# Diagonal masks of the transposed causal scores: from VectorE to TensorE in every third head group

## What is computed

```python
xn1 = layernorm(x, g1, be1)
q, k, v = heads(xn1 @ Wq + bq), heads(xn1 @ Wk + bk), heads(xn1 @ Wv + bv)   # 16 heads of 32
scores = einsum('bhtd,bhsd->bhts', q, k) / DH ** -0.5
scores = where(tril(ones(1024, 1024)), scores, -inf)      # causal
sa = einsum('bhts,bhsd->bhtd', softmax(scores), v)
x = x + (sa @ W1 + b1)
x = x + cross_attention(layernorm(x), ctx) @ W2 + b2       # 64 context rows, no mask
x = x + relu(layernorm(x) @ Wf1 + bf1) @ Wf2 + bf2
out = layernorm(x + gate(x) * routed_vision(x))            # fusion stage
```

## Time and profile before

| | us |
|---|---|
| runs | 2347.75, 2347.81, 2345.16; median 2347.75 |
| profiled execution: span, first to last instruction | 2338.9 |
| median less span | 8.85 |
| TensorE busy | 2198.0 (94%) |
| VectorE busy | 1410.1 (60%) |
| POOL busy | 933.6 (40%) |
| ScalarE busy | 868.2 (37%) |
| mask additions on VectorE (L1011), 512 | 138.3 |

### The profile page before, as it was taken

The page is one execution under the profiler, slowest core; times in us unless marked ns, Lnnn a source line. Parts: engine busy times, 40 slices in busy tenths (PEclk is TensorE's granted clock), DMA queues, the critical chain, the costliest instruction groups (busy, mean ns, idle before and its releaser), DMA issues.

```text
span 2338.9 us, 31417 instructions
## 1 busy us (share of the span) xinstructions
PE 2198.0 (94%) x11206; PEld 1595.5 (68%) x11206; DVE 1410.1 (60%) x3349; ACT 868.2 (37%) x1598; POOL 933.6 (40%) x943
## 2 busy tenths in 40 slices
PE   7999999999999998789999998999999999999996
PEld 5655565556555654447777776788887887888784
DVE  5477757875786566735666668453455546454646
ACT  3155545654565455533443334321111122112213
POOL 1068657766777577773333333010111202011212
PEclk9999999999999998789999999999999999999998
DMA  7465545553556356212111121321112121212011
GB/s 231 55 93 97 92 71 77 103 93 62 83 97 97 60 88 124 69 56 85 59 55 55 59 95 55 113 86 36 50 54 75 52 82 44 87 55 68 33 36 50
DMA packets 106320, 177.29 MB, mean 76 GB/s; under 512 B 18334, under 2 KB 23454, under 8 KB 106160
## 3 DMA queue, kind: packets, MB, share of 16 engines
q1 hardware_dynamic: 106164, 175.29, 32.4%
HBM read 83.67 MB, written 40.13 MB: 53 GB/s over the span
## 4 chain that ended last, share of the span: by engine, by line
PE 75%; DVE 9%; issue 6%; ACT 4%; POOL 3%; DMA 2%; SPq 0%; POOLq 0%; ACTq 0%; DVEq 0%
PE psum L55 18%; PE psum L56 17%; PE psum L57 17%; PE psum L797 5%; PE psum L745 5%; PE psum L785 4%; PE psum L806 2%; DMA small<-es 2%; PE psum L703 1%; DVE psum L1000 1%; POOL es L660 1%; ACT sx L1346 1%; PE psum L1300 1%; DVE mx L1004 1%; PE psum L1292 1%
## 5 line engine op out<-in xcount | busy, mean ns | idle before, releaser
L660 POOL TENSOR_TENSOR es<-es,er 128x512 f32<-128x512 f32 (+3 forms) x640 | 589.6, 961 | 322.5 <-PE psum L797 283.4
L895 ACT ACTIVATE er<-psum 128x512 f32<-128x512 f32 (+3 forms) x640 | 280.4, 470 | 316.0 <-DVE psum L1011 181.2
L1000 DVE CUSTOM_DVE_ANT_0 psum<-psum,mask_ts 128x384 f32<-128x384 f32 (+3 forms) x512 | 247.9, 500 | 201.2 <-PE psum L745 200.5
L785 PE MATMUL psum<-qs,ks 100*128 100x512 f32 (+3 forms) x768 | 264.5, 377 | 17.1 <-DVE mx L1004 6.6
L745 PE MATMUL psum<-ks,qs 96*128 96x512 f32 (+3 forms) x768 | 267.2, 373 | 10.9 <-DVE mx L1000 6.6
L1850 ACT ACTIVATE fy<-psum,cols 128x512 f32<-128x512 f32 x128 | 88.2, 689 | 451.4 <-PE psum L57 450.9
L745 PEld LDWEIGHTS psum<-ks,qs 96*128 96x128 f32 x768 | 144.0, 194 | 109.7 <-issue 39.4
L1004 DVE TENSOR_REDUCE mx<-psum 128x1 fp32r<-128x512 f32 x256 | 175.1, 684 | 60.7 <-PE psum L745 59.8
L785 PEld LDWEIGHTS psum<-qs,ks 100*128 100x128 f32 x768 | 145.9, 196 | 92.4 <-DVE mx L1004 23.1
L55 PE MATMUL psum<-fh,hh 128*128 128x512 f32 x512 | 201.1, 393 | 7.1 <-DVE hl L1951 7.1
L55 PE MATMUL psum<-fah,fh 128*128 128x512 f32 x512 | 202.6, 396 | 0.0
(11 more groups left out here) (258 smaller groups left out, 4479.8 us busy)
## 6 DMA issues: line engine op xcount, KB each, us to landing
qs<-stage SPq DMA_DIRECT2D x96, 256.0 KB, 5.7
ks<-stage SPq DMA_DIRECT2D x96, 256.0 KB, 6.9
rs<-rs_d SPq DMA_DIRECT2D x32, 256.0 KB
sa_d<-rs SPq DMA_DIRECT2D x32, 256.0 KB, 2.2
sx<-sa_d SPq DMA_DIRECT2D x8, 1024.0 KB, 5.7
xt<-in_x SPq DMA_DIRECT2D x32, 256.0 KB, 6.1
x_d<-xt SPq DMA_DIRECT2D x32, 256.0 KB, 2.0
fw<-in_Wf SPq DMA_DIRECT2D x16, 512.0 KB, 5.3
```

Of the source, the lines that this page charges most:

```text
L660: e.tensor_tensor(es, es, er, ALU.add).then_inc(s_add.sem, 1)
L785: t = e.matmul(ps[:, off:512], Q.ks[par][0:100, i, 128 * j:128 * j + 128], Q.qs[par][0:100, i, 512 * c2 + off:512 * c2 + 512], start=True, ...
L895: e.activation(dst, bank1("sc", g, c2, j, i)[:, off:512], ACT.Exp, scale=SCALE).then_inc(s_freeS.sem, 1)
L1000: t = e.tensor_tensor_reduce(out=ps, in0=ps, in1=mask_ts[:, 512 - wd:512], scale=1.0, scalar=-3e38, op0=ALU.add, op1=ALU.max, accum_out=mx ...
```

## The change

In groups with g % 4 == 2 the mask is added by TensorE: behind the score product into the same PSUM bank comes a second product, identity by `mask_st`, onto the tile's first 128 columns, accumulating. VectorE's `low` step disappears in these groups, and the exponential waits for TensorE alone and is planned 0.001 behind the score. `mask_st` becomes an fp32r tile, which VectorE reads as float32 in the other groups; it lies over memory that `ag`, `rw` and a filler use, so that no other tile moves. The masks still made by VectorE are counted by `Q.low`.

```diff
+def masked_by_pe(g):
+    return g % 4 == 2
...
-                if s[0] == "sc" and s[3] >= 4 * c2:
+                if s[0] == "sc" and s[3] >= 4 * c2 and not masked_by_pe(g):
                     t += [(at + 0.014, ("low", *s[1:])), (at + 0.028, ("ex", *s[1:]))]
                 elif s[0] == "sc":
                     t.append((at + 0.001, ("ex", *s[1:])))
...
-        mask_st = sb(top, "mask_st", [128, 128], BF16)
+        with ExitStack() as ctx:
+            mask_st = sb(ctx, "mask_st", [128, 128], F32R)
         ag = sb(top, "ag", [128, NB, 8])
         rw = sb(top, "rw", [128, NB, 8])
+        sb(top, "spare", [128, 64])
...
+            if s[0] == "low":
+                Q.low[s[1:]] = len(Q.low)
...
-                    e.memset(mask_st[:], 0.0).then_inc(s_const.sem, 1)
+                    e.memset(mask_st[:].bitcast(F32), 0.0).then_inc(s_const.sem, 1)
...
+                    diag = masked_by_pe(g) and j >= 4 * c2
                     t = e.matmul(ps[:, off:512], Q.ks[par][0:100, i, 128 * j:128 * j + 128],
-                                 Q.qs[par][0:100, i, 512 * c2 + off:512 * c2 + 512], start=True, stop=True)
+                                 Q.qs[par][0:100, i, 512 * c2 + off:512 * c2 + 512], start=True, stop=not diag)
+                    if diag:
+                        w.wait_ge(s_const, 6)
+                        t = e.matmul(ps[:, off:off + 128], identr[:], mask_st[:], start=False, stop=True)
                     t.then_inc(s_fillS.sem, 1)
...
-                    if j >= 4 * c2:
-                        w.wait_ge(s_low, 32 * g + 4 * j + i + 1)
+                    if j >= 4 * c2 and not masked_by_pe(g):
+                        w.wait_ge(s_low, Q.low[g, c2, j, i] + 1)
                     else:
                         w.wait_ge(s_fillS, Q.useS["sc", g, c2, j, i] + 1)
...
-                    e.tensor_tensor(ps, ps, mask_st[:], ALU.add).then_inc(s_low.sem, 1)
+                    e.tensor_tensor(ps, ps, mask_st[:].bitcast(F32), ALU.add).then_inc(s_low.sem, 1)
```

More of the change, by code:

```diff
@@ L423, in program @@
         O1 = [s for _, s in O1]
-        Q.useA, Q.useP, Q.useM, Q.useS, Q.outS, Q.slot, Q.pv = {}, {}, {}, {}, {}, {}, {}
+        Q.useA, Q.useP, Q.useM, Q.useS, Q.outS, Q.slot, Q.pv, Q.low = {}, {}, {}, {}, {}, {}, {}, {}
         for s in O1:
@@ L631, in pool1 @@
                     w.wait_ge(s_const, 4)
-                    e.affine_select(out=mask_st[:], in_=mask_st[:], compare_op=ALU.is_ge, fill=NEG, base=0,
+                    e.affine_select(out=mask_st[:], in_=mask_st[:].bitcast(F32), compare_op=ALU.is_ge, fill=NEG, base=0,
                                     pattern=[[1, 128]], channel_multiplier=-1).then_inc(s_const.sem, 1)
```

## The result

The changed kernel took 2354.09 us (median of 9 runs, 2347.53 to 2359.57), beside 2347.20 for the kernel before (9 runs, 2340.08 to 2349.60). The ratio is 1.0027, with a 95% interval of 1.0014 to 1.0039: slower by about 6.3 us, on the far side of the 0.2% that the prediction set as the border to no change. (The ratios here do not come from the two medians alone; they differ from theirs by up to 0.0006.) The forecast was 2351. The masks that moved are those of the third of every four groups (2, 6, 10 and 14), which is one group in four and not in three, as the title could be read.

A forecast was written before the change was run, and what follows sets the result against it. In the changed groups it took a DMA landing before the reciprocal to bound first halves, and POOL's additions to decide late in second halves. 0 + 0 + 2.4 + 1.0 = +3.4 us; 2338.9 + 8.85 + 3.4 = 2351, range 2337.5 to 2359.

The forecast's parts named there:

- First halves, "Worth 0": Queries 0 to 511 of the changed groups: VectorE's up to 4.48 us saved only lengthens the reciprocal's DMA wait; worth 0.
- "Its start, counted from the group's, stays": Groups 2, 6, 10: the reciprocal starts as before, while the wait before it grows from 1.3 to some 4 us.
- Mask products, 0.12 each: TensorE behind each diagonal score: 0.12 us per added product, 3.8 a group, 15.4 in all, none carried by the path.
- Rival D: The mask product costs near its upper bound, 0.3 us instead of 0.12, and eats the covers: 2367 us; chance 0.06.
- Plan, 0: Exponentials planned 1.5 us sooner, 228 of 1,664 bank uses with another predecessor, planned distances hardly moved: counted 0.
- Second halves, 0: Second halves of the changed groups: 4.23 us of masks less on VectorE, under POOL's gapless 18.78 us run; worth 0.
- Eviction order, +2.4: Group's end: key eviction falls behind the last exponential, the following small DMA 0.8 us later; three groups, +2.4 us.
- Group 14, +1: POOL's additions hold VectorE's long subtraction out longer, less vanished masks and POOL work done: net +1 us, bounds +5.2, -8.4.
- Rival B: Group 14: the long subtraction gets in between two POOL additions; -6.0 us in all, 2341.7; chance 0.13.
- Rival C: Group 14, 941 to 956: POOL keeps VectorE out longer than lost masks give back; +10.5 us in all, 2358; chance 0.24.
- Rival A: First halves shorten because the reciprocal is no wall; -10.2 us, 2337.5; chance 0.12.
- The base, "8.85 above the span": Whole kernel: the runs' median lies 8.85 us above the profiled span of 2338.9, as start and end around it.

The follow-up runs named there:

- no_product: The changed kernel with the masks of groups 2, 6, 10, 14 left out altogether, no added product; 2353.84 us, ratio 1.0019 to the kernel before.
- wall_moved: The changed kernel with part of the next group's maximum pass, the reciprocal and the copies behind it planned later; 2364.14 us, ratio 1.0077 to the kernel before.
- wide_mask: The changed kernel's 32-bit mask tile and memory overlay, but all masks on VectorE in their old places; 2344.46 us, ratio 0.9987 to the kernel before.
- move_only: All masks on VectorE with the 32-bit tile, but masks and exponentials of groups 2, 6, 10, 14 planned directly behind the score; 2347.55 us, ratio 1.0002.
- half1_only: The change in the first halves (queries 0 to 511) of groups 2, 6, 10, 14 alone; 2355.67 us, ratio 1.0038 to the kernel before.
- va_b: The kernel before with two small layer norm operations of stage 1 done by POOL in place of VectorE; 2348.94 us, ratio 1.0011 to the kernel before.
- order_kept: The changed kernel, but exponentials of diagonal tiles in groups 2, 6, 10, 14 keep their old place in the plan; 2354.38 us, ratio 1.0022.
- half2_only: The change in the second halves of groups 2, 6, 10, 14 alone; 2351.87 us, ratio 1.0027 to the kernel before.
- half2_again: The same program as half2_only, run again for a second trace and twelve more times; 2351.42 us, ratio 1.0021 to the kernel before.
- fill: The changed kernel plus twelve unused 512-column products ahead of TensorE's wait for the key copies in groups 2, 6, 10; 2347.20 us, ratio 1.0006.
- va_f: The changed kernel with the twelve filling products of fill and the two small layer norm operations on POOL; 2343.84 us, ratio 0.9992 to the kernel before.
- va_h2: The change in the second halves alone, with the two small layer norm operations on POOL; 2346.07 us, ratio 0.9999 to the kernel before.

## Why the prediction was right or wrong

**The size came near (2351 for 2354.09), and that is luck.** The sum's +3.4 us were 2.4 for the eviction order, whose price turned out as nothing, and 1.0 for group 14. The measured 6.3 us or so are mostly of a kind that has no term in the sum. By the prediction's own split the outcome, over 0.2% slower, belongs with C and D (0.30) and not with the forecast (0.45).

**First halves, "Worth 0": the step that failed.** Its two halves must be told apart. The cover was right: the reciprocal is a wall, and its wait grew from 1.31, 1.22 and 0.95 us to 4.67, 3.80 and 4.88 in groups 2, 6 and 10, as foretold (some 4). The price was wrong: I asked what the path gains when VectorE gets ahead, and not what TensorE does then. It finished its work ahead of the landing 2.0 us sooner (pass of values j = 3 at 13.09 us of group 2 against 15.11) and stood still for 3.4. Of the +4.9 us of group 2, 0.8 came at the border, 2.7 in the stretch behind it that ran at half clock, and the rest around a second stretch at half clock (0.50 granted from 262.1 to 268.9, which the kernel before has for half as long).

**"Its start, counted from the group's, stays": wrong by a microsecond.** It moved from 16.67, 15.83, 16.36 us to 17.63, 16.75, 17.83. The key copies and the small transfer land later though they are issued as early in the group (6.85 against 6.80 us in group 2). The DMA engines are full in that stretch in both (share 0.96 and 1.08 at 143 to 145 GB/s, windows above). One thing in the traces bears on it. TensorE transposes the next element's rows earlier in the changed kernel, and that frees their buffer, so SP issues two loads of rows sooner (lines of the kernel before, then after):

```profile
232.74 0.81 SPq L572 DMA_DIRECT2D xr<-in_x  x2
232.23 0.81 SPq L580 DMA_DIRECT2D xr<-in_x  x2
```

Counted from the starts of groups 2, 6 and 10 that is 13.2 to 14.0 us before and 12.0 after, while the key copies are still on their way. Over the 14 traces the last key copy of groups 2, 6 and 10 lands at 16.4 us on average where the loads were issued ahead of 13 us (20 places), and at 16.0 where behind (22 places), each with a scatter of 0.5. So these loads may carry a part of the delay; no run held them back, and the cause stays open.

**The wall was drawn with one waiter too few.** I took it from VectorE's wait alone. TensorE's own wait for the keys is not in the trace of before, because the copies landed 0.1 to 0.4 us ahead of its product there (product at 16.07 us of group 2, last landing at 15.99).

**Mask products, 0.12 each: right** (0.11), and most of the loss is there without them, as no_product shows; its interval (1.0004 to 1.0033) leaves room for a small share. Rival D is out. **Wide mask, 0: right.** **Plan, 0: right.**

**Second halves, 0: not settled.** POOL's run kept its length to 0.01 us, as foretold. (The first mask of the stretch, at 256.96 before, starts just ahead of that run; nothing hangs on it.) Alone they cost 5 us all the same, and nothing that can be measured with the small operations on POOL.

**Eviction order, +2.4: mechanism right, price 0.** The eviction moved, and the small transfer behind it is issued 0.7 to 0.8 us later in groups 7 and 11 (7.35 and 7.41 us into the group, against 6.66 and 6.65) and 1.8 later in group 3. Groups 7 and 11 still last 67.3 and 67.4 us, as before: the later landing is covered.

**Group 14, +1: mechanism right, size not contradicted.** The subtraction took 14.15 us, inside the 13 to 15 given; the group itself was 0.8 us shorter than in the one trace before. Over the traces but wall_moved's (12.27) it splits by one thing. Where VectorE masks the second half of group 14, it took 6.75 to 10.91 us (before, wide_mask, move_only, half1_only, va_b), and the group 65.3 us on average. Where not, 13.7 to 15.0 (change, order_kept, no_product, half2_only, half2_again, fill, va_f, va_h2), and 66.7: +1.4, or +0.9 without order_kept's 70.5. Rival B would need 1.3. The Trainium skill's rule ("SBUF — State Buffer", section "Who interferes with whom") says that the instruction that issues first has the shared ports for its whole length and the other is blocked; I took it to mean a wait of one addition. These waits, and the 4.17 us beside POOL's unbroken additions, are longer: VectorE got its turn when POOL paused, not between two additions. The short cases agree with that reading: in group 1 of the kernel before the small operation starts at 35.41 us, POOL's running addition ends at 35.82 and the operation at 35.85.

**Rival C** had the sign and, at +10.5, a place that is not it: group 14 carries about 1 us. **Rival A** is out: groups 2, 6 and 10 are longer by 2 to 5 us, none at 54 or less.

**The base, "8.85 above the span": wrong.** Only 1.8 us lie around the span. The profiled execution was 6.5 us faster than the median; how much of that lies in its clock and how much in lockouts was not worked out. The sum against the median stood because both errors were one and the same number.

## What to carry to other kernels

Ahead of a transfer that sets the end, taking work off another engine is not free, as the first halves show: it can pull the matmul engine's scattered idle time together, and then the work behind the wait is dearer than the wait. Ask of each wall who stands before it after the change, and how long each of them stands still in one piece; a row of otherwise useless matmuls ahead of the wait is a cheap test (12 of them took the ratio from 1.0027 to 1.0006 here, some 5 us of 6.3). Compare single traces only where the code differs, and check how far untouched stretches differ as well.

## What the runs showed of the hardware

- The clock: behind 12 of 12 gaps of 2.01 to 3.84 us between two starts of TensorE it was granted at half for 3.4 to 6.8 us. In the changed kernel 35, 47 and 38 products were then issued in 10 us, against 53, 53 and 55 in the kernel before.
- The lockout: a VectorE operation on 128x2 elements in SBUF, 0.15 to 0.17 us when POOL is quiet, took 0.54 or 4.17 us in two executions of one program. In half2_only and fill VectorE reached it at the same 35.42 us of group 1, with POOL's additions 0.03 us apart (one starts at 33.37 and 33.34), and the operation took 4.17 and 0.47 us. The place within POOL's addition does not tell the two outcomes apart in the traces: 0.62 and 0.81 us into it VectorE was locked out (half1_only, half2_only), 0.55, 0.67, 0.77 and 0.83 us into it it got in (no_product, order_kept, half2_again, fill). What decides is open.
- Groups 1, 5 and 9, of unchanged code, sum to 155.2 to 167.0 us over the traces. Clock and lockouts are the candidates seen for the scatter of the whole (2340 to 2350 us in 9 runs of the kernel before); their shares were not measured.
